# Inverse H transform of a spectral convolution on one core: one 128-column matmul per channel against two 64-column matmuls

## The chip, the cores and the metric

The kernel runs on one NeuronCore of a Trainium2 chip. The metric is device time in microseconds (us) of one execution, taken as the median of several. A profiled execution of the same program gives the trace from which all rows below come. The engines are called as the profile calls them: PE is TensorE's matmul side and PEld its weight loads, DVE is VectorE, ACT is ScalarE, POOL is GpSimd, SP is the engine that issues the large transfers.

## The reference

The input `x` has shape (4, 128, 128, 768) in float32: 4 images of 128 by 128 pixels with 768 channels. The channels form 8 blocks of 96. What is computed, cut to what matters:

```python
xf = jnp.fft.rfft2(x, axes=(1, 2), norm='ortho')          # over H and W
...                                                         # per block of 96 channels, complex:
o1r = relu(xr @ w1[0] - xi @ w1[1] + b1[0]); o1i = relu(xi @ w1[0] + xr @ w1[1] + b1[1])
o2r = o1r @ w2[0] - o1i @ w2[1] + b2[0];     o2i = o1i @ w2[0] + o1r @ w2[1] + b2[1]
o2r, o2i = softshrink(o2r, 0.01), softshrink(o2i, 0.01)
out = jnp.fft.irfft2(o2r + 1j * o2i, s=(H, W), axes=(1, 2), norm='ortho') + x
```

## The kernel before

The work is cut into 32 units, which this text calls images: one unit is one of the 4 input images with one block of 96 channels. All transforms are matmuls against cosine and sine tables held in `tab`. A loop of 16 steps runs over pairs of units; inside a step the two units (`p` = 0 and 1) are written out one after the other. Every engine has its own program, and semaphores alone tie them together.

For each unit PE goes through four stages in a fixed order that is written out by hand:

- **Forward lines** (`forward_lines`, lines 434 and 435): one matmul against row 0 of the image (line 418), and then for each of the 96 channels the transform along W. The stationary operand is a channel's 128 by 127 slice, held in one of five `ring` buffers. It is already issued as two matmuls: columns 0 to 63 of the slice give output partitions 0 to 63, columns 64 to 126 give partitions 64 to 126.
- **Mixing** (lines 468 to 561): the forward H transform (`fwd_big`, line 468, whose stationary operands have 128 columns, and `fwd_small`, line 480, which writes two halves of 64 partitions), the two complex products with ReLU between them, bias and softshrink on DVE. Near its end `keep_warm` (line 567) issues a few matmuls whose result nobody reads.
- **Inverse lines** (`inverse_lines`, line 447): for each of the 96 channels the inverse transform along H. The stationary operand is a channel's 128 by 128 slice in a `ring` buffer, the moving operand is the table `inv_h` of 128 columns. This stage is what the change touches.
- **Rows** (`rows`, lines 574 and 577): the inverse transform along W, 13 groups of two matmuls with up to 480 moving columns.

The 96 channels of a line stage are cut into 26 groups: 22 of 4 channels, then 3, 2, 2 and 1. One group fills one PSUM bank. For every group three things happen. ACT or DVE packs the channels from `ydg` into a `ring` buffer (ACT line 632, DVE line 767; the first five groups by ACT line 657 and, for the first 12 slots, DVE line 894). PE then multiplies and raises `line_done` on the group's last matmul. ACT or DVE moves the bank back into `ydg` (ACT line 638, DVE line 773). PE waits before group g for its pack, and from group 8 on for the move of group g - 8; a pack of group g waits for PE's group g - 5. After the last group `lines_moved` makes PE wait until all moves are done, since `rows` reads all of `ydg`. In the rows stage DVE (lines 839, 848 and 855) and POOL (line 926) add the results to the image, and SP stores them as they come and then loads the image after next into the same buffer.

In the program's rows each matmul of float32 stands once, while the trace shows it as two LDWEIGHTS and two MATMUL records. So 32 units of 96 channels make 6144 records of a kind.

Of the kernel before, what the change touches and what calls it, by code (L numbers as in the profile page):

```python
# [17 lines left out]
HALF = 64  # L18
# [16 lines left out]
RING = 5  # L35
# [6 lines left out]
def packer_h(g):  # L42
    return "act" if g < RING or g % 3 == 2 else "dve"
# [8 lines left out]
def upto(owner, g, who):  # L52
    return sum(owner(i) == who for i in range(g + 1))
# [124 lines left out]
def build(nc, x, mix, table, out):  # L178
    with ExitStack() as ctx:
        def sb(name, shape, dt=F32):  # L180
            return ctx.enter_context(nc.sbuf_tensor(name, shape, dt))
# [27 lines left out]
        ring = [sb(f"ring{j}", [128, CG, 128]) for j in range(RING)]  # L209
        ps = ctx.enter_context(nc.psum_tensor("ps", [128, 8, 512], F32))  # L210
# [53 lines left out]
        def mat(name):  # L264
            a, b = COLS[name]
            return tab[:, a:b]
# [17 lines left out]
        def line_bank(stage, g):  # L284

            return (g + ROW0_BANK + 1) % 8 if stage == 0 else g % 8
# [7 lines left out]
        def wait_moved(engine, q, stage, g):  # L294
            who = mover(stage, g)
            engine.wait_ge(line_sems[who], moved_count(q, stage, g, who))
# [70 lines left out]
        with nc.Block() as block:  # L367
# [46 lines left out]
            def _(pe):  # L414
# [23 lines left out]
                def inverse_lines(q):  # L438
                    for g in range(NG):
                        if g >= 8:  # L440
                            wait_moved(pe, q, 1, g - 8)
                        who = packer_h(g)
                        pe.wait_ge(pack_sems[who], PACKED_H[who] * q + upto(packer_h, g, who))
                        if g < RING:
                            pe.wait_ge(tail_packed, RING * q + g + 1)
                        for j in range(LINE_GROUPS[g][1]):
                            mm = pe.matmul(ps[:, line_bank(1, g), j * 128:(j + 1) * 128], ring[g % RING][:, j, :],  # L447
                                           mat("inv_h"), start=True, stop=True)
                        mm.then_inc(line_done, 1)

                def lines_moved(q, stage):
# [131 lines left out]
                with pe.Fori(0, STEPS) as t:  # L583
                    for p in range(PAIRS):
# [31 lines left out]
                        merge(q)  # L616
                        keep_warm(q, 3)
                        inverse_lines(q)
                        lines_moved(q, 1)
                        for g in range(NF):  # L620
# [327 lines left out]
```

## Time and profile before

| | |
|---|---|
| runs | 5172.28 us median of 3 (5172.27 to 5175.37) |
| profiled execution, its own time | 5172.48 us |
| its span from the first to the last instruction | 5170.2 us |
| PE busy | 5031.5 us, 97% of the span |
| PEld busy | 4143.5 us, 80% |
| DVE busy | 3993.2 us, 77% |
| ACT busy | 2508.0 us, 49% |
| POOL busy | 627.2 us, 12% |
| mean granted TensorE clock | 0.999 |

Busy time of PE is the union of matmul records. Records overlap (one begins before the one ahead of it has ended), so that a busy engine can still have its work done faster; what counts is the distance from one start to the next.

### The profile page before, as it was taken

What the parts mean: (1) busy time and instruction counts of PE and PEld (TensorE: products, weight loads), DVE (VectorE), ACT (ScalarE), POOL (GpSimd) and SP (SyncE); (2) the same over time, 40 slices, a digit from 0 to 9 for tenths busy, and PEclk for the clock granted to TensorE, in tenths of its full rate; (3) what the DMA queues carried; (4) which work ended last, traced back from release to release, by engine and by line L of the source; (5) the groups of instructions that cost most, each with busy time, mean ns of one, the idle gap of its engine ahead of it and who ended that gap; (6) DMA issues with size and microseconds to landing.
All of it is one profiled execution on the core that took longest, in us unless ns stands there. A gap on an engine that the chain in (4) does not pass through costs nothing.

```text
span 5170.2 us, 111909 instructions
## 1 busy us (share of the span) xinstructions
PE 5031.5 (97%) x43072; PEld 4143.5 (80%) x43072; DVE 3993.2 (77%) x5987; ACT 2508.0 (49%) x3649; POOL 627.2 (12%) x420
## 2 busy tenths in 40 slices
PE   7999999999999999999999999999999999999999
PEld 6887878888787887878878887888878778887887
DVE  6778777787777877778777787777787777877777
ACT  4554544545455454554445544445445455454543
POOL 0111011110111101111011110011110111101111
PEclk9999999999999999999999999999999999999999
DMA  3331233312333113332133321333312333123311
GB/s 107 99 99 36 73 100 99 104 44 61 100 99 104 50 54 99 99 104 61 44 100 99 104 74 43 87 99 104 89 41 74 99 104 99 44 61 99 103 50 50
DMA packets 1067748, 421.11 MB, mean 81 GB/s; under 512 B 1064864, under 2 KB 1064992, under 8 KB 1067168
## 3 DMA queue, kind: packets, MB, share of 16 engines
q1 hardware_dynamic: 1062432, 411.63, 30.1%
q8 instruction: 382, 6.26, 0.5%
q10 hardware_dynamic: 4736, 1.60, 0.1%
q14 instruction: 198, 1.62, 0.1%
HBM read 210.26 MB, written 201.33 MB: 80 GB/s over the span
## 4 chain that ended last, share of the span: by engine, by line
issue 88%; POOL 12%; POOLq 0%; DVE 0%
POOL x L926 12%; POOLq L925 0%; POOLq L929 0%; DVE x L855 0%; POOLq L926 0%; POOLq L938 0%
## 5 line engine op out<-in xcount | busy, mean ns | idle before, releaser
L926 POOL TENSOR_TENSOR x<-shrink_or_v,x 128x480 f32<-128x480 f32 (+1 forms) x416 | 627.0, 1507 | 4534.8 <-DVE shrink_or_v L848 4494.8
L543 PE MATMUL ps<-wts,hbig 128*128 128x192 f32 x4160 | 734.9, 327 | 4.3
L820 DVE TENSOR_TENSOR shrink_or_v<-ps,wts 128x768 f32<-128x768 f32 (+1 forms) x544 | 501.0, 921 | 281.5 <-PE ps L552 254.7
L773 DVE COPY ydg<-ps 128x512 f32<-128x512 f32 (+5 forms) x768 | 504.5, 657 | 250.8 <-PE ps L447 151.8
L447 PE MATMUL ps<-tab,ring 128*128 128x128 f32 x6144 | 694.6, 276 | 0.0
L447 PEld LDWEIGHTS ps<-tab,ring 128*128 128x128 f32 x6144 | 688.5, 192 | 5.4 <-DVE ring L894 5.4
L543 PEld LDWEIGHTS ps<-wts,hbig 128*128 128x128 f32 x4160 | 671.4, 190 | 16.5 <-ACT hbig L688 13.7
L434 PE MATMUL ps<-tab,ring 128*64 128x128 f32 x6144 | 681.6, 274 | 2.4 <-ACT ring L628 2.4
L435 PE MATMUL ps<-tab,ring 128*63 128x128 f32 x6144 | 681.6, 274 | 0.0
L434 PEld LDWEIGHTS ps<-tab,ring 128*64 128x64 f32 x6144 | 672.2, 137 | 7.3 <-ACT ring L628 4.2
L435 PEld LDWEIGHTS ps<-tab,ring 128*63 128x63 f32 x6144 | 672.1, 136 | 0.0
L638 ACT COPY ydg<-ps 127x512 f32<-127x512 f32 (+5 forms) x896 | 504.9, 573 | 344.2 <-PE ps L435 173.4
L665 ACT COPY zbig<-ps 128x512 f32<-128x512 f32 (+1 forms) x544 | 308.8, 568 | 613.6 <-PE ps L468 611.2
L468 PEld LDWEIGHTS ps<-tab,ydg 128*128 128x128 f32 x4032 | 506.1, 191 | 105.5 <-issue 84.3
L468 PE MATMUL ps<-tab,ydg 128*128 128x128 f32 x4032 | 567.4, 282 | 19.2 <-DVE ydg L773 17.7
L798 DVE TENSOR_TENSOR zlo<-zbig,zhi 128x1024 fp32r<-128x1024 f32 (+1 forms) x320 | 326.2, 1019 | 258.0 <-ACT zhi L672 258.0
L830 DVE TENSOR_TENSOR ydg<-shrink_or_v 128x768 f32<-128x768 f32 (+2 forms) x544 | 489.3, 899 | 17.8
L688 ACT ACTIVATE hbig<-ps,wts 128x1024 f32<-128x1024 f32 (+1 forms) x320 | 305.5, 955 | 310.0 <-PE ps L526 310.0
L628 ACT COPY ring<-x 128x508 f32<-128x508 f32 (+1 forms) x416 | 435.0, 1080 | 9.2 <-PE ps L435 9.2
L679 ACT CAST zsmall_hi<-ps 128x512 fp32r<-128x512 f32 (+1 forms) x320 | 163.1, 510 | 564.1 <-PE ps L480 564.1
L574 PE MATMUL ps<-ydg,tab 128*128 128x480 f32 (+1 forms) x832 | 396.0, 558 | 14.8 <-DVE ydg L773 14.8
L577 PE MATMUL ps<-ydg,tab 128*128 128x480 f32 x832 | 402.9, 566 | 0.0
(71 smaller groups left out, 7507.0 us busy)
## 6 DMA issues: line engine op xcount, KB each, us to landing
out<-x SPq DMA_DIRECT2D x352, 480.0 KB, 4.6
x<-in_x SPq DMA_DIRECT2D x192, 768.0 KB, 7.9
x<-in_x SPq DMA_DIRECT2D x32, 816.0 KB, 8.1
x<-in_x SPq DMA_DIRECT2D x32, 720.0 KB, 6.4
out<-x SPq DMA_DIRECT2D x32, 432.0 KB, 4.2
wts<-in_mix SPq DMA_DIRECT2D x16, 513.0 KB, 3.6
out<-x SPq DMA_DIRECT2D x32, 240.0 KB, 4.4
out<-x SPq DMA_DIRECT2D x32, 192.0 KB, 4.3
```

The lines of the kernel that those rows point to most:

```text
L434: pe.matmul(o[0:HALF], slot[:, 0:HALF], mat("fwd_w"), start=True, stop=True)
L435: mm = pe.matmul(o[HALF:127], slot[:, HALF:127], mat("fwd_w_odd"), start=True, stop=True)
L447: mm = pe.matmul(ps[:, line_bank(1, g), j * 128:(j + 1) * 128], ring[g % RING][:, j, :], mat("inv_h"), start=True, stop=True)
L468: mm = pe.matmul(ps[:, z_bank(u, h), k * H:(k + 1) * H], t[:, s:s + 2, :].rearrange("p k c -> p (k c)")[:, 0:BIG], mat("fwd_h"), start=Tru ...
L543: mm = pe.matmul(o, hbig[:, k * H:(k + 1) * H], mix_part("w2_big"), start=first, stop=False, skip_group_check=True)
L577: pe.matmul(ps[:, bank, 0:HG * CB], mat("inv_w_even"), ydg[:, HG * g:HG * g + HG, :].rearrange("p h c -> p (h c)"), start=True, stop=True) ...
L628: act.copy(*line_pack_moves(p, g)).then_inc(line_packed_act, 1)
L638: act.copy(*line_moves(stage, g)).then_inc(line_act, 1)
L773: dve.tensor_copy(*line_moves(stage, g)).then_inc(line_dve, 1)
L820: dve.tensor_tensor(parts(v), d, b2, ALU.add).then_inc(bias_done, 1)
L830: dve.tensor_tensor(dst, parts(v)[:, :, first:ne, :], parts(c)[:, :, first:ne, :], ALU.subtract).then_inc(shrunk, 1)
L926: pool.tensor_tensor(xs[p][:, a:b, :], ucopy[g % 4][:, 0:b - a, :], mirror(xs[p], a, b), ALU.add).then_inc(plus_ready, 1)
```

## The change

Each channel's matmul of the inverse H transform is issued as two: columns 0 to 63 of the channel's slice as the stationary operand, with output partitions 0 to 63 of the bank, and columns 64 to 127 with output partitions 64 to 127. Both read the same moving operand, the whole table `inv_h`. The semaphore is raised by the group's last matmul, as before. No other line changes; from the next line on, line numbers are one higher.

```diff
                         if g < RING:
                             pe.wait_ge(tail_packed, RING * q + g + 1)
                         for j in range(LINE_GROUPS[g][1]):
-                            mm = pe.matmul(ps[:, line_bank(1, g), j * 128:(j + 1) * 128], ring[g % RING][:, j, :],
-                                           mat("inv_h"), start=True, stop=True)
+                            for half in (slice(0, HALF), slice(HALF, 128)):
+                                mm = pe.matmul(ps[half, line_bank(1, g), j * 128:(j + 1) * 128],
+                                               ring[g % RING][:, j, half], mat("inv_h"), start=True, stop=True)
                         mm.then_inc(line_done, 1)
```

How the rows of PE's program stand at the place where the stage begins, behind the unread matmuls (`ps<-tab`), in the kernel before; "64x128" is output partitions by moving columns, and a count stands where rows repeat:

```order
L567 MATMUL ps<-tab 128x128 [waits zsmall_ready]
L567 MATMUL ps<-tab 128x128 x2
L443 ISA
L445 ISA [waits packed_act]
L447 MATMUL ps<-tab,ring 128x128 [waits tail_packed]
L447 MATMUL ps<-tab,ring 128x128 x3
```

The same place of PE's program after the change:

```order
L568 MATMUL ps<-tab 128x128 [waits zsmall_ready]
L568 MATMUL ps<-tab 128x128 x2
L443 ISA
L445 ISA [waits packed_act]
L448 MATMUL ps<-tab,ring 64x128 [waits tail_packed]
L448 MATMUL ps<-tab,ring 64x128 x7
```

The first group's 4 matmuls of 128 output partitions are 8 of 64 now, and the waits stand where they stood. At the end of the stage PE's program reads in the kernel before (the last group has one channel, and the row behind it begins the rows stage):

```order
L443 REGISTER_ALU [waits line_dve]
L447 MATMUL ps<-tab,ring0 128x128 [waits packed_dve]
L453 REGISTER_ALU
L453 REGISTER_ALU [waits line_act]
L574 MATMUL ps<-ydg,tab 128x384 [waits line_dve]
```

And after the change:

```order
L443 REGISTER_ALU [waits line_dve]
L448 MATMUL ps<-tab,ring0 64x128 [waits packed_dve]
L448 MATMUL ps<-tab,ring0 64x128
L454 REGISTER_ALU
L454 REGISTER_ALU [waits line_act]
L575 MATMUL ps<-ydg,tab 128x384 [waits line_dve]
```

Here too one matmul has become two between the same waits.

## Rows read from the trace of the kernel before

**Rows 1.** The page's parts 1 and 3: engines' busy time, and DMA queues.

```profile
PE 5031.5 (97%) x43072; PEld 4143.5 (80%) x43072; DVE 3993.2 (77%) x5987; ACT 2508.0 (49%) x3649; POOL 627.2 (12%) x420
...
q8 instruction: 382, 6.26, 0.5%
```

**Rows 2.** Groups by line, whole run: xcount | busy us, mean ns | idle before.

```profile
L447 PE MATMUL ps<-tab,ring 128*128 128x128 f32 x6144 | 694.6, 276 | 0.0
...
L434 PE MATMUL ps<-tab,ring 128*64 128x128 f32 x6144 | 681.6, 274 | 2.4 <-ACT ring L628 2.4
L435 PE MATMUL ps<-tab,ring 128*63 128x128 f32 x6144 | 681.6, 274 | 0.0
```

**Rows 3.** Timeline of PE, inverse lines of one unit: start us, us, what.

```profile
311.16 0.83 PE L567 MATMUL ps<-tab 128*128 128x128 f32 x6
311.96 21.70 PE L447 MATMUL ps<-tab,ring 128*128 128x128 f32 x192
334.13 0.59 PE L574 MATMUL ps<-ydg,tab 128*128 128x384 f32 x1 [0.46 <-DVE ydg L773]
```

**Rows 4.** Timeline of PE, the next unit's forward lines, begin and end.

```profile
355.55 0.32 PE L434 MATMUL ps<-tab,ring 128*64 128x128 f32 x1
355.56 0.32 PE L435 MATMUL ps<-tab,ring 128*63 128x128 f32 x1
355.71 0.27 PE L434 MATMUL ps<-tab,ring 128*64 128x128 f32 x1
...
376.46 0.27 PE L435 MATMUL ps<-tab,ring 128*63 128x128 f32 x1
377.29 0.37 PE L468 MATMUL ps<-tab,ydg 128*128 128x128 f32 x1 [0.56 <-DVE ydg L773]
```

**Rows 5.** Timeline of PE in mixing: 128 columns, then halves of 64, then 128.

```profile
378.84 0.50 PE L468 MATMUL ps<-tab,ydg 128*128 128x128 f32 x3
379.26 1.09 PE L480 MATMUL ps<-tab,ydg 128*64 128x128 f32 x16
380.29 0.49 PE L468 MATMUL ps<-tab,yedge 128*128 128x128 f32 x2
```

**Rows 6.** Timeline of DVE and ACT where the inverse lines begin.

```profile
311.71 0.66 DVE L894 COPY ring<-ydg 128x48 f32<-128x48 f32 x5 [0.15 <-ACT ydg L726]
...
314.79 1.10 ACT L632 COPY ring<-ydg 128x512 f32<-128x512 f32 x1
```

**Rows 7.** Timeline of DVE where the inverse lines end.

```profile
333.04 1.04 DVE L773 COPY ydg<-ps 128x256 f32<-128x256 f32 x2 [0.43 <-PE ps L447]
```

**Rows 8.** Windows, both line stages: PE, PEld, DVE, ACT, POOL busy, clock, DMA share, GB/s.

```profile
311.96:334.13 22.17, 21.71 (x193) 21.51 (x192) 16.69 (x31) 16.20 (x24) 0.00 (x0) 1.00 0.09 26
355.55:377.29 21.74, 21.18 (x386) 20.93 (x385) 17.17 (x31) 15.94 (x25) 2.96 (x2) 1.00 0.97 249
```

**Rows 9.** Waits, whole run: us in total, times, longest us.

```profile
ACT ydg L638 <- PE ps L447: 170.8, 256, 1.1
DVE ydg L773 <- PE ps L447: 151.8, 288, 1.7
...
PE ps L574 <- DVE ydg L773: 14.8, 32, 0.5
...
PE ps L418 <- DVE shrink_or_v L848: 1.6, 9, 0.2
```

**Rows 10.** Timeline of PE, starts of the stage in three other units (windows cut the counts).

```profile
152.17 1.05 PE L447 MATMUL ps<-tab,ring 128*128 128x128 f32 x7
...
472.46 0.71 PE L447 MATMUL ps<-tab,ring 128*128 128x128 f32 x4
...
632.27 0.94 PE L447 MATMUL ps<-tab,ring 128*128 128x128 f32 x6
```

## The prediction

> **What bounds the kernel now.** I read the page first: PE is busy 97% of the span, the next engine, DVE, 77% [rows 1]. PE being busy doesn't say that it couldn't go faster, so I went to the groups by line and then to the timeline of PE through one unit. The reader is to see there that the inverse lines are one unbroken run of 192 records over 21.70 us, and that over all 32 units PE was idle before them for 0.0 us [rows 2, 3]. The waits say the same from the other side: within this stage it is the movers that wait for PE, ACT 170.8 us and DVE 151.8 us in total, some 5 us per unit each [rows 9]. The windows agree: of the stage's 22.17 us DVE works 16.69 and ACT 16.20 [rows 8]. So the stage lasts as long as PE takes to issue its matmuls, plus a tail: the stage's last move ends, and only then PE begins the rows (0.46 us idle, waiting for DVE line 773) [rows 3, 7]. What PE saves in the stage is time saved, as long as nobody else becomes late by it.
>
> **What the change costs and gives.** It takes 6144 matmul records of 128 stationary columns away and puts 12288 of 64 columns in their place; each still streams 128 moving columns. No DMA, no work of DVE, ACT, POOL or SP is added or moved.
>
> The kernel before holds nearly the same code: the forward lines do 96 channels as pairs of 64 and 63 stationary columns out of the same ring, against a table of 128 columns. There the two halves start 0.01 us apart and run beside each other, so a pair costs about one slot of time and not two [rows 4]. The run goes from 355.55 to the end of its last record, 376.46 + 0.27 = 376.73: 21.18 us, for the same 96 channels that take 21.70 us as whole matmuls [rows 3, 4]. Difference 0.52 us per unit.
>
> I want to know where this comes from, since a difference between two stages could be due to something else in them. Forward: the second pair starts at 355.71, 0.16 after the first, and the last of the 192 pairs about at 376.45, so the other 190 steps take 20.74 us: 0.1092 each [rows 4]. Inverse: the last record starts some 0.275 before the end (mean duration 276 ns [rows 2]), at 21.43 into the run. Its first step is not seen alone in that row, but line 468 in mixing has the same shape, and there two records of a run that starts unprepared last 0.49 us together, so that the second starts 0.49 - 0.275 = 0.21 after the first [rows 5]. That leaves 21.22 us for 190 steps: 0.1117 each. So the pair saves 2.5 ns in each of 190 steps, 0.47 us, and 0.05 us in the first step.
>
> Could the tables matter? The forward pairs use two different tables and the inverse pairs one table twice. Line 480 in mixing has that form: 16 records, 8 pairs against one table, in 1.09 us [rows 5]. With 0.16 for the first step, 6 steps of 0.109 and a last record of 0.28 it comes to 1.09. The pair's step is the same. The one column that the forward's second half lacks (63 against 64) is also complete there, and costs nothing that shows.
>
> **The entry.** PE now goes from whole matmuls (the unread ones) to halves, and back at the end; before, it did neither here. Mixing shows what such a turn costs: the last of line 468's records starts at 378.84 + 0.50 - 0.275 = 379.06, the first half-width one at 379.26, that is 0.20 later where a step of 0.11 would be usual [rows 5]. At the entry of the inverse lines the last unread matmul starts at 311.16 + 0.83 - 0.275 = 311.71 and the first inverse one at 311.96, already 0.25 later [rows 3]. What holds it is DVE's first tail pack: five of them take 0.66 us from 311.71 on, so that the first is done near 311.91 [rows 6]. The turn's 0.20 us lies under that wait; it would be exposed by some 0.2 us only if the two came one after the other. I take nothing for the entry; bounds 0 and 0.09 us (0.20 less the usual 0.11).
>
> The Trainium skill says of the same thing, in "TensorEngine Tiling (Array Packing)", section "Key Properties", that changing the tiling mode drains the engine, which speaks against a change that adds two such turns per unit. The trace agrees that such a turn costs time (0.20 us against 0.11 [rows 5]). If both were paid in full on top of the waits, the sum would shrink to the case "both turns exposed" below.
>
> **The exit.** From halves to whole: the last line 480 record starts at 379.26 + 1.09 - 0.27 = 380.08, the first whole one at 380.29, 0.21 later [rows 5]. At the end of the inverse lines PE stands idle for 0.46 us anyway until DVE has moved the last bank [rows 3], so the turn is hidden. The last half starts 0.01 us behind its partner, and the last move can begin only then: a loss of 0.01 us. The forward stage has a longer tail, 377.29 - 376.73 = 0.56 us [rows 4], of which 0.1 us more than the inverse stage's. It is followed by other waits in the program (row 0's transfer, the edges), so I count it against nothing, but as the pessimistic bound of the tail I take it whole: 0.10 us.
>
> **Who becomes late.** The closest of the packs is ACT's first, for group 5: it ends at 314.79 + 1.10 = 315.89 [rows 6]. PE needs it after 40 records: today at 311.96 + 0.21 + 39 x 0.1117 = 316.53 for the matmul and about 0.11 earlier for its weights, 316.42. After the change at 311.96 + 0.05 + 39 x 0.109 = 316.27 for the weights. 0.38 us are left of 0.53. From then on a stage shorter by 0.5 us has to fit DVE's 16.69 and ACT's 16.20 us into 21.65, while the forward stage already fits 17.17 and 15.94 into 21.74 with 2.4 us of PE idle in the whole run [rows 2, 8]. The wait behind the stage moves with it: rows begin when the last bank is moved, and DVE's chain of the rows stage, for which PE's line 418 waits (1.6 us in all [rows 9]), begins with the first row matmul. Stores and loads are released by the same chain and shift as a whole. Nothing in the loop is tied to a time of its own, so the saving of a unit is a saving of the run.
>
> **The sum.** 21.70 - 21.18 = 0.52, less 0.01 at the exit: 0.51 us per unit, x 32 = 16.3 us. From the profiled execution's own 5172.48 us (span 5170.2) this gives 5156.2, and from the median of 5172.28, which lies 0.2 below it, **5156.0 us**, a change of 0.32%. A measurement of this kernel can tell about 0.2%, 10.3 us, from no change. Bounds of the parts: entry 0 to 0.09, exit 0.01 to 0.10, together at worst 0.18 us of loss more, which is 5.8 us.
>
> **The rivals.**
> 1. Both turns exposed. The 0.20 us of a turn add themselves to the waits instead of lying under them. Gain 0.51 - 0.18 = 0.33 us per unit, 10.6 us: 5161.7. For it speaks that the first inverse record waits for a semaphore that its weight load carries; against it that in mixing the turn takes place with no wait at all, so it needs no semaphore to begin [rows 5]. Chance 0.07.
> 2. The pair runs at the whole matmul's step, 0.1117, because each half streams the same 128 columns and the step is set by something that a pair doesn't shorten. Only the first step's 0.05 us less the 0.01 of the exit stays, 1.3 us: 5171. Two stretches of the trace in this form run at 0.109 [rows 4, 5], which speaks against it. Chance 0.05.
>
> The same page's section "Theoretical Speedup" gives a gain only where a dimension is 64 or less, and a whole 128 by 128 slice cut in two has none; by that the time would be rival 2's. The trace disagrees, if only by 2.5 ns per step.
>
> 3. ACT or DVE become late in the stage: pack 5 has 0.38 us left. If another unit's early packs came later than in the one read, PE would wait part of its saving away. The idle time of 0.0 us over 32 units [rows 2] says that no unit comes near. Gain halved, 8 us: 5164. Chance 0.03.
> 4. Slower: PE runs out of instructions. Instructions are themselves brought in while the kernel runs (6.26 MB on one queue [rows 1]), and the inverse lines follow mixing, which is dense already, while the forward lines, with the same density as the new stage, follow the sparse rows stage and may live on what was fetched during it. A place where the supply breaks off is the turn of the loop: a unit takes 311.96 - 152.17 = 159.79 us, one with the turn in it 472.46 - 311.96 = 160.50, the next 632.27 - 472.46 = 159.81 [rows 3, 10], so a turn costs 0.7 us. One such stall per inverse stage would give 0.7 - 0.51 = 0.2 us of loss per unit, 6 us: 5178, and two 5201. It decides from 0.51 us per unit on. Against it: the forward stage keeps the density for 21 us while DMA is 97% busy, whereas in the inverse stage it is 9% [rows 8]. Chance 0.03.
>
> **How the numbers follow.** The forecast has 0.82, rivals 0.07, 0.05, 0.03 and 0.03. The range of 5153 to 5162 holds the forecast, with 3 us below it for parts that the reading in hundredths of a us hides (0.1 us per unit), and rival 1 above: 0.89 of the cases, of which I believe 0.8 after errors of my own reading. Faster by over 0.2% are the forecast and, at the very bound, half of rival 1: 0.85. Within 0.2%: the other half, rival 2 and rival 3, 0.12. Slower: 0.03.
>
> **What would show it.** The line's matmul group should be 12288 records, still with no idle time ahead of it, of about 273 ns; a run of them in one unit about 21.2 us long, with starts of pairs 0.109 apart; its first start 0.25 after the last unread matmul's start, as now; and the rows' wait for DVE at 0.46 to 0.48 us. All other stages keep their lengths: a unit takes 159.3 and 160.0 us in turn. The prediction is wrong if the pair's step is not that of the forward lines, if the entry grows, or if idle time appears in front of a later stage by as much as this one lost.

## The result, and the profile after

| | before | after |
|---|---|---|
| median | 5172.85 us (5171.31 to 5175.37, 8 runs) | 5156.97 us (5156.48 to 5158.11, 8 runs) |
| profiled execution | 5172.48 us, span 5170.2 | 5156.87 us, span 5154.6 |

The ratio is 0.9969, with a 95% interval of 0.9958 to 0.998: 15.9 us less. The forecast was 5156.0 with a range of 5153 to 5162.

The groups by line of after, whole run, answer to [rows 2]; the columns are the same.

```profile
L434 PE MATMUL ps<-tab,ring 128*64 128x128 f32 x6144 | 681.8, 273 | 2.8 <-ACT ring L629 2.8
L435 PE MATMUL ps<-tab,ring 128*63 128x128 f32 x6144 | 681.8, 273 | 0.0
L448 PE MATMUL ps<-tab,ring 128*64 128x128 f32 x12288 | 677.8, 273 | 0.0
L448 PEld LDWEIGHTS ps<-tab,ring 128*64 128x64 f32 x12288 | 670.1, 137 | 5.4 <-DVE ring L895 5.4
```

Line 448 is the old line 447. It has twice the records and 16.8 us less busy time (694.6 before), and still no idle time ahead of it. Its busy time per unit is now the forward lines' 21.18 us.

The timeline of PE in the same unit as [rows 3]:

```profile
310.81 0.83 PE L568 MATMUL ps<-tab 128*128 128x128 f32 x6
311.62 21.18 PE L448 MATMUL ps<-tab,ring 128*64 128x128 f32 x384
333.27 0.91 PE L575 MATMUL ps<-ydg,tab 128*128 128x384 f32 x2 [0.47 <-DVE ydg L774]
```

The reader is to see three distances. From the last unread matmul's start (310.81 + 0.83 - 0.275 = 311.37) to the first half it is 0.25 us, as before. The run is 21.18 us long and not 21.70. The idle time in front of the rows is 0.47 us and not 0.46.

The starts of the stage in the two units behind it answer to [rows 10] (windows cut the counts):

```profile
471.53 0.66 PE L448 MATMUL ps<-tab,ring 128*64 128x128 f32 x8
...
630.82 0.88 PE L448 MATMUL ps<-tab,ring 128*64 128x128 f32 x12
```

From one stage to the next it is 471.53 - 311.62 = 159.91 us with the loop's turn in it and 159.29 without; before it was 160.50 and 159.81.

The waits of after, where they answer to [rows 9], with two that are small:

```profile
ACT ydg L639 <- PE ps L448: 156.3, 256, 1.0
...
DVE ydg L774 <- PE ps L448: 141.0, 288, 1.6
...
PE ps L418 <- DVE shrink_or_v L849: 2.6, 12, 0.3
```

The movers wait for PE 25.3 us less than before (170.8 + 151.8 against 156.3 + 141.0), and still wait for it: PE bounds the stage as it did.

### The profile page after: what moved, and what is told of

Same layout as the page of the kernel before. It is cut to its first block, busy times and chain, and to the rows that moved or that the text cites. A ratio compares the mean times of both kernels' runs of the same rounds, so it can differ in the third digit from the quotient of the medians.

```text
span 5154.6 us, 124197 instructions
## 1 busy us (share of the span) xinstructions
PE 5015.0 (97%) x49216; PEld 4124.6 (80%) x49216; DVE 3992.1 (77%) x5987; ACT 2507.4 (49%) x3649; POOL 627.3 (12%) x420
## 4 chain that ended last, share of the span: by engine, by line
issue 88%; POOL 12%; POOLq 0%; DVE 0%
POOL x L927 12%; POOLq L926 0%; POOLq L930 0%; DVE x L856 0%; POOLq L927 0%; POOLq L939 0%
## 5 line engine op out<-in xcount | busy, mean ns | idle before, releaser
L774 DVE COPY ydg<-ps 128x512 f32<-128x512 f32 (+5 forms) x768 | 504.4, 657 | 240.0 <-PE ps L448 141.0
L434 PE MATMUL ps<-tab,ring 128*64 128x128 f32 x6144 | 681.8, 273 | 2.8 <-ACT ring L629 2.8
L434 PEld LDWEIGHTS ps<-tab,ring 128*64 128x64 f32 x6144 | 671.5, 137 | 8.5 <-ACT ring L629 4.8
L448 PE MATMUL ps<-tab,ring 128*64 128x128 f32 x12288 | 677.8, 273 | 0.0
L448 PEld LDWEIGHTS ps<-tab,ring 128*64 128x64 f32 x12288 | 670.1, 137 | 5.4 <-DVE ring L895 5.4
```

The costliest lines, as they stand in the source:

```text
L434: pe.matmul(o[0:HALF], slot[:, 0:HALF], mat("fwd_w"), start=True, stop=True)
L448: mm = pe.matmul(ps[half, line_bank(1, g), j * 128:(j + 1) * 128], ring[g % RING][:, j, half], mat("inv_h"), start=True, stop=True)
L774: dve.tensor_copy(*line_moves(stage, g)).then_inc(line_dve, 1)
```

## The experiments

Two questions were open behind a forecast that came true. Why is a pair of halves 2.5 ns faster than a whole matmul (theory A: a whole's step is set by loading 128 stationary columns; theory B: a fixed cost in each pass)? And does the turn from whole to half matmuls cost something that DVE's wait only hides? Each run was timed beside the kernel before on its own chip; that kernel's median was 5174.6 us beside e1 to e4, 5173.3 beside e5 to e8 and 5173.4 beside e9 to e12. e1, e2, e5, e6 and e7 stand on one execution each, the others on five or more.

**e1: one half alone.** The kernel of after, where the upper half of each channel's slots is not computed in this stage:

```diff
-                            for half in (slice(0, HALF), slice(HALF, 128)):
+                            for half in (slice(0, HALF),):
```

> The kernel of after with only the first half (columns 0 to 63) of each channel issued in the inverse lines; the second half's output is left out. Theory A (a whole record's step of 0.1117 us is set by loading its 128 stationary columns, a half's step of 0.109 by streaming its 128 moving columns, so that a second half beside the first costs nothing): one half alone still steps at 0.109, the stage is 21.17 us and the kernel at 5157 us, within 1 us. Theory B (there is a fixed cost of 2.5 ns in each of the two passes of a record, and a pair hides one of them by overlap): a half alone has nothing beside it and steps at 0.1117, the stage is 21.65 us, the kernel near 5172 us. Theory C (the two halves take turns and share the step): the stage falls clearly below 21 us, until DVE with 16.7 us of work in it bounds it.

5157.38 us. The timeline of PE in e1:

```profile
311.55 21.18 PE L448 MATMUL ps<-tab,ring 128*64 128x128 f32 x192
```

Half the records take the same 21.18 us. The second half of after costs nothing, and the step of a lone half is already the short one. This is A's number; B wanted 21.65 and C less than 21.

**e2: whole matmuls, 96 moving columns.** The kernel of before; 32 of the 128 columns of each channel's result are left out:

```diff
-                            mm = pe.matmul(ps[:, line_bank(1, g), j * 128:(j + 1) * 128], ring[g % RING][:, j, :],
-                                           mat("inv_h"), start=True, stop=True)
+                            mm = pe.matmul(ps[:, line_bank(1, g), j * 128:j * 128 + 96], ring[g % RING][:, j, :],
+                                           mat("inv_h")[:, 0:96], start=True, stop=True)
```

> The kernel of before (whole matmuls) with 96 of the 128 moving columns in the inverse lines; the other 32 columns of each channel's result are left out. Theory A (the load of 128 stationary columns sets the step): the step stays at 0.1117 us and the stage at 21.7 us, the kernel at 5172 us. Theory B (streaming plus 2.5 ns in each of two passes): the step is 0.080 + 0.005 = 0.085 us, a group of 4 channels takes 0.68 us, and the stage goes down until DVE and ACT bound it, to 17 to 18 us; the kernel gets 120 to 150 us faster.

5173.22 us. The timeline of PE in e2:

```profile
312.24 21.68 PE L447 MATMUL ps<-tab,ring 128*128 128x96 f32 x192
```

A quarter of the streaming is gone and the stage is 0.02 us shorter. Streaming does not set the step of a whole matmul of 128 columns.

**e5: halves, 96 moving columns.** The same cut in the kernel of after:

```diff
-                                mm = pe.matmul(ps[half, line_bank(1, g), j * 128:(j + 1) * 128],
-                                               ring[g % RING][:, j, half], mat("inv_h"), start=True, stop=True)
+                                mm = pe.matmul(ps[half, line_bank(1, g), j * 128:j * 128 + 96],
+                                               ring[g % RING][:, j, half], mat("inv_h")[:, 0:96], start=True, stop=True)
```

> The kernel of after (halves) with 96 of the 128 moving columns in the inverse lines; the other 32 columns of each channel's result are left out. Theory A (a whole's step is set by its load of 128 columns, a half's by streaming): the step falls to 0.080 + 0.0025 = 0.0825 us, where the whole matmuls stayed at 0.112 with the same 96 columns. PE would need 15.9 us for the stage, DVE and ACT have more than 16 in it, so the stage ends at 17 to 18 us and the kernel near 5157 - 32 x 3.7 = 5040 us. Rival (the halves' step is set by their own load or by the issue of four records): the step stays at 0.109 and the kernel at 5157.

5015.51 us. The timeline of PE in e5, in a unit that begins some 4 us earlier:

```profile
307.09 3.52 PE L448 MATMUL ps<-tab,ring 128*64 128x96 f32 x80
311.04 12.76 PE L448 MATMUL ps<-tab,ring 128*64 128x96 f32 x304 [0.43 <-ACT ring L633]
324.32 0.91 PE L575 MATMUL ps<-ydg,tab 128*128 128x384 f32 x2 [0.52 <-DVE ydg L774]
```

The second run of 304 records, 152 pairs, takes 12.76 us; less the last record of 0.25 and a first step of some 0.13, that leaves 12.38 us for 150 steps, 0.0825 us, the number expected. The same cut that gave whole matmuls nothing gives halves a quarter. The stage is 17.23 us; PE runs into a wait of 0.43 us for ACT's pack 5. The expected 5040 was too careful: DVE and ACT held PE up there once, and not for the rest of the stage. The pack is the one that the prediction named as the closest.

Taken together, e1, e2 and e5 leave only theory A of the three: the step of a whole matmul is the load of its 128 columns, 0.112 us, and that of a half is its streaming, 0.109 us with 128 moving columns and 0.0825 with 96. The experiments vary the streaming and not the load alone, but the rows of the weight loads show the load. In the kernel before, and in e7 (quarters, below):

```profile
L447 PEld LDWEIGHTS ps<-tab,ring 128*128 128x128 f32 x6144 | 688.5, 192 | 5.4 <-DVE ring L894 5.4
```

```profile
L448 PEld LDWEIGHTS ps<-tab,ring 128*32 128x32 f32 x24576 | 673.1, 110 | 36.0 <-issue 28.4
```

The mean record is 110 ns for 32 columns, 137 for 64 (the result's rows above) and 192 for 128: 27 ns more for 32 columns, 55 for 64. That is 0.85 ns a column and, as an estimate from these rows, 0.11 us for 128, the step of a whole matmul.

**e3 and e4: 6 unread matmuls instead of 3**, in the kernel of before and of after:

```diff
-                        keep_warm(q, 3)
+                        keep_warm(q, 6)
```

> The kernel of before with 6 unread matmuls ahead of the inverse lines instead of 3, so that DVE's tail pack is done before PE is through with them. Both theories: the first inverse record follows the last unread one by one step, 0.11 us, and its own step is 0.11 instead of 0.21: 6 records of 0.1117 are added (0.67 us), 0.14 of waiting and 0.10 of the first step are saved: 0.43 us per unit, 13.8 us, 5186 to 5187.

> The kernel of after with 6 unread matmuls instead of 3. Theory (the turn from whole to half matmuls costs 0.20 us from start to start and lies under DVE's wait in the kernel of after): the turn is exposed now. First half 0.20 after the last unread start, so 0.67 - 0.05 = 0.62 us more per unit, 19.8 us, 5176.8; the gain over the whole matmuls with 6 unread ones falls from 16 to about 9.5 us. Rival (a turn costs nothing, and what mixing shows at line 480 is something else): the first half follows after 0.11, 0.53 us more per unit, 5173.9, gain 12.4 us. Second rival (the turn is already paid on top of the wait in the kernel of after): gain stays near 16 us or grows.

e3 5187.48 us (ratio 1.0025, 1.0015 to 1.0035), e4 5177.69 us (1.0006, 0.9996 to 1.0016). The timeline of PE in e3:

```profile
311.86 1.50 PE L567 MATMUL ps<-tab 128*128 128x128 f32 x12
313.20 3.07 PE L447 MATMUL ps<-tab,ring 128*128 128x128 f32 x26
```

And in e4:

```profile
312.11 1.50 PE L568 MATMUL ps<-tab 128*128 128x128 f32 x12
313.54 0.66 PE L448 MATMUL ps<-tab,ring 128*64 128x128 f32 x8
```

With DVE's wait out of the way the first whole record starts 313.20 - (311.86 + 1.50 - 0.275) = 0.11 us after the last unread one, the first half 313.54 - (312.11 + 1.50 - 0.275) = 0.20 us. So the turn is real, it costs 0.09 us, and in the kernel of after it lies wholly under the wait. Exposed, it cuts the gain from 15.9 to 9.8 us, where 9.5 was expected. That is not the turn alone: in e3 the first step of the whole matmuls has become short as well.

**e6: halves apart.** Within a group the lower halves of all its channels, and then the upper ones:

```diff
-                        for j in range(LINE_GROUPS[g][1]):
-                            for half in (slice(0, HALF), slice(HALF, 128)):
+                        for half in (slice(0, HALF), slice(HALF, 128)):
+                            for j in range(LINE_GROUPS[g][1]):
```

> The kernel of after with the halves in another order: within a group first the lower halves of all channels, then the upper ones. Theory (two halves run beside each other only when neighbours in the program use different columns of the array): each half takes a step of its own, but for the neighbours at the borders of runs. 384 records less some 51 borders, at 0.109, is 36.4 us, without the borders 41.9: the stage grows by 15 to 21 us, the kernel to 5640 to 5820. Rival (PE finds the partner in its queue by itself): 5157.

5248.49 us, a miss by over 390 us. The timeline of PE in e6: the stage's beginning in two windows that end at 314.774 and 314.79, and the whole run:

```profile
314.28 0.76 PE L448 MATMUL ps<-tab,ring 128*64 128x128 f32 x5
...
314.28 0.82 PE L448 MATMUL ps<-tab,ring 128*64 128x128 f32 x6
...
314.28 24.05 PE L448 MATMUL ps<-tab,ring 128*64 128x128 f32 x384
```

The group has 8 records of lower halves before the first of an upper half. Five have started by 314.774, and a sixth starts before 314.79, although a record of the same columns would follow 0.109 later, near 314.88. So, by this spacing, the first upper half begins beside the fifth lower one, ahead of three records that stand before it in the program. If all halves took their own steps, the stage would last 384 x 0.109 = 41.9 us; it lasts 24.05, 2.87 more than with neighbours paired, which is about one step of 0.11 for each of the 25 borders between groups. PE finds the partner by itself, at some steps' distance, and the order of halves matters far less than expected.

**e7: quarters.**

```diff
-                            for half in (slice(0, HALF), slice(HALF, 128)):
+                            for half in (slice(0, 32), slice(32, 64), slice(64, 96), slice(96, 128)):
```

> The kernel of after with four matmuls of 32 stationary columns per channel. Theory A: streaming 128 columns still sets the step, and the four quarters run beside each other, as they start 0.01 us apart: step 0.109, 5157 within 2 us, or up to 1 us per stage more for the later start of the last quarter. Rival (PE can't issue eight records in 0.109 us, or instructions don't come in fast enough with 24576 more of them): the step grows; at 0.02 us per record it would be 0.16, 10 us per unit, 5470.

5192.04 us, between the two. What the weight loads and the matmuls of line 448 wait for without a releaser, over the whole run of e7 (us in total, times, longest us):

```profile
PEld ps L448 <- issue: 28.4, 70, 0.9
PE ps L448 <- issue: 11.1, 39, 0.6
```

And one unit's timeline; its window begins behind the stage's first 8 records:

```profile
152.76 12.61 PE L448 MATMUL ps<-tab,ring 128*32 128x128 f32 x448
165.52 7.25 PE L448 MATMUL ps<-tab,ring 128*32 128x128 f32 x248 [0.16 <-issue]
172.93 1.96 PE L448 MATMUL ps<-tab,ring 128*32 128x128 f32 x64 [0.15 <-issue]
```

While it runs, it runs as theory A says: 448 records are 112 steps, and (12.61 - 0.27) / 111 = 0.111 us, with one short delay in it. But here PE stops, waiting for nothing that the profile shows: its weight loads 70 times for 28.4 us in all, its matmuls, which come out of the same stops later, 39 times for 11.1 us. The stage takes 22.26 us on average instead of 21.18, 34 us more in 32 units, which is nearly all of what e7 loses. No run of halves has such stops. They stand at fixed places: here behind record 8 + 448 = 456 of the stage and behind 456 + 248 = 704. In a unit of the loop's other half:

```profile
954.67 17.22 PE L448 MATMUL ps<-tab,ring 128*32 128x128 f32 x618
972.19 3.69 PE L448 MATMUL ps<-tab,ring 128*32 128x128 f32 x124 [0.30 <-issue]
976.06 1.07 PE L448 MATMUL ps<-tab,ring 128*32 128x128 f32 x26 [0.18 <-issue]
```

In all units of the first kind the stops are behind records 456, 580 or 704, in all of the other behind 370, 494, 618 or 742: multiples of 124 apart. The queue that brings instructions ([rows 1]) moves 526 packets in e7 and 430 in the kernel of after, 96 more for 12288 more MATMUL records, which is one packet for 128 of them. Within the stage its packets start 3.8 us apart in e7's trace (median over all units), while 124 records at full pace take 31 steps of 0.109, 3.4 us; in the kernel of after they start 7.0 us apart. All this fits the rival of the prediction that PE runs out of instructions; that it is what PE waits for is inferred, since the profile names no releaser.

**e8: turns merged.** With a turn priced at 0.09 us plus its first step, this run moves turns instead of adding them. Halves stand now also next to halves that were there: the forward H transform of iteration 0, the first part of iteration 1, all second parts, and the second product in the loop.

```diff
-                        mm = pe.matmul(ps[:, z_bank(u, h), k * H:(k + 1) * H],
-                                       t[:, s:s + 2, :].rearrange("p k c -> p (k c)")[:, 0:BIG], mat("fwd_h"),
-                                       start=True, stop=True)
+                        for part in ((slice(0, HALF), slice(HALF, BIG)) if u == 0 or h == 1 or (u, h) == (1, 0)
+                                     else (slice(0, BIG),)):
+                            mm = pe.matmul(ps[part, z_bank(u, h), k * H:(k + 1) * H],
+                                           t[:, s:s + 2, :].rearrange("p k c -> p (k c)")[:, part], mat("fwd_h"),
+                                           start=True, stop=True)
...
-                                mix2_whole(q, it - 2)
+                                mix2_whole(q, it - 2, (slice(0, HALF), slice(HALF, H)))
```

> The kernel of after, with halves also for the forward H transform's first iteration, for the first part of the second one and for every second part, and for the product behind them (the one of 192 moving columns) inside the loop, so that a turn from whole to half matmuls moves forward instead of being added, and one per unit falls away. Theory (turn 0.09 us and 0.05 us of first step, and 2.5 ns for each whole record of 128 moving columns replaced, none for those of 192, whose streaming of 0.160 us is longer than the load): 0.14 + about 90 records x 0.0025 = 0.36 us per unit, 11.7 us: 5145 to 5146. Rival (halves next to row-tiled or accumulating matmuls cost more than seen): at or above 5157.

5182.95 us (ratio 1.0018, 1.0009 to 1.0027), 37 us worse than expected. Two windows of e8 around the same wait in mixing, in two units; the columns are those of [rows 8], and the first number behind POOL is the granted clock:

```profile
223.00:227.00 4.00, 3.34 (x9) 2.28 (x9) 0.61 (x2) 0.00 (x0) 0.00 (x0) 0.69 1.08 295
383.00:387.00 4.00, 2.13 (x11) 1.61 (x9) 1.83 (x2) 0.99 (x3) 0.00 (x0) 1.00 1.17 325
```

And its timeline of PE in the first of them:

```profile
223.66 0.50 PE L497 MATMUL ps<-zhi,w1lo 128*128 128x512 f32 x1 [1.87 <-DVE zsmall_lo L805]
224.00 0.39 PE L498 MATMUL ps<-zhi,w1hi 128*128 128x512 f32 x1
...
225.68 0.63 PE L510 MATMUL ps<-zsmall_hi,w1lo 128*128 128x512 f32 x1
226.11 0.63 PE L511 MATMUL ps<-zsmall_hi,w1hi 128*128 128x512 f32 x1
```

PE sat idle for 1.87 us, and 0.85 us after it had begun again its matmuls took 0.43 us from start to start instead of 0.23: the clock stood at the 1.2 GHz level, which the window shows as 0.69 on average. It happened behind this wait in 19 of 32 units, which took 1.5 us longer; in the others it stayed at 2.4 GHz, though the wait is 1.87 us in all 32. In the kernel of after the same wait is 1.50 us and the clock never falls there. The edit had made PE arrive earlier at a result that DVE delivers when it does, and so made the wait longer.

**e9: e8 with 6 unread matmuls in that wait.**

```diff
+                            if it == 1:
+                                for i in range(6):
+                                    pe.matmul(ps[:, SMALL_BANK, 0:H], mat("inv_h"), mat("fwd_h"), start=True, stop=True)
                             if it >= 1:
                                 mix1_whole(q, it - 1)
```

> The kernel of run e8 (turns merged) with 6 more unread matmuls (12 records of 128 columns, 1.3 us) in PE's wait of 1.87 us for the first remainder of DVE, line 805 there. In e8 19 of 32 units had the clock at 1.2 GHz for 3.4 us right behind that wait and took 1.5 us longer; the others took 0.21 us less than in the kernel of after. Theory (the longer idle time let the clock fall, and nothing else is wrong with e8): granted clock back at 0.999 and all units 0.21 us shorter than after's, 5149 to 5151. Rival (the fall has another cause, as the halves themselves): the clock falls again and the time stays near 5180.

5156.66 us (ratio 0.9967, 0.9955 to 0.9979), the clock back at 0.999, 26.3 us less than e8. The 26 us were the fall of the clock. But of the 6.7 us that were expected beyond the gain of after, next to nothing came. The waits of e9 say where it stopped:

```profile
DVE x L764 <- issue: 29.4, 27, 2.4
...
PE ps L471 <- DVE zsmall_lo L808: 5.9, 13, 1.0
```

And the timeline of DVE in e9:

```profile
391.15 1.06 DVE L764 TENSOR_TENSOR x<-x 128x864 f32<-128x864 f32 x1 [2.44 <-issue]
```

Line 764 is the first fold of the next image. The expectation of e12 takes this idle time for a wait for that image's first rows, but in the trace these had landed at 373.93, 17 us earlier. What stands there is the turn of DVE's own loop (line 921), between these two instructions:

```profile
L921 DVEq COMPARE_BRANCH  x1: 63/63/63, 387.5 to 387.5; - x1
L921 DVEq FUSED_REGOPS  x1: 62/62/62, 391.0 to 391.0; - x1
```

The first is the branch at the loop's end, the second the first instruction of the loop's body, 3.6 us later. e9's trace has 14 such turns of 2.8 to 3.6 us, and DVE's idle time in them is 25.4 us, most of the 29.4 above. The turn comes in every second unit. Behind it DVE has three folds to do, and the remainder for PE's line 471, which follows them, is late.

**e10: only the late merges**, iterations 2 to 6:

```diff
-                        for part in ((slice(0, HALF), slice(HALF, BIG)) if u == 0 or h == 1 or (u, h) == (1, 0)
+                        for part in ((slice(0, HALF), slice(HALF, BIG)) if h == 1 and u >= 2
```

> The kernel of e8 without its edits to the first two iterations: halves only in the second parts of iterations 2 to 6 of the forward H transform, and in the second product inside the loop. PE's wait for the first remainder is as in after, 1.5 us, so the clock stays at 0.999. Theory: 5 parts of 8 whole records become 8 steps of halves, 0.0025 us less each, 0.1 us per unit, 3 us: 5153 to 5155. Rival (the second product's halves, beside accumulating into the same bank, cost more): at or above 5157.

5158.07 us (ratio 0.997, 0.9958 to 0.9981), span of the profile 5154.6, the same as after's. The clock stayed up, as expected, but the 3 us didn't come; the interval is too wide to show 3 us, the trace is not. Units without DVE's loop turn are 0.1 us shorter, as expected (159.20 us from one stage to the next against 159.29), so the second product's halves cost nothing there. The other units lose it:

```profile
PE ps L471 <- DVE zsmall_lo L805: 8.8, 11, 1.3
```

In after's trace this wait is 0.4 us. DVE's first fold waits 34.5 us in all in e10's trace, where it is 25.9 in after's: the loop's turn took 3.4 us on average, and 2.8 in after. Why it took longer is not shown.

**e11: more turns.** The kernel of after, with halves in the first parts of iterations 2 to 9, which stand between row-tiled and whole matmuls:

```diff
-                        mm = pe.matmul(ps[:, z_bank(u, h), k * H:(k + 1) * H],
...
+                        for part in ((slice(0, HALF), slice(HALF, BIG)) if h == 0 and u >= 2 else (slice(0, BIG),)):
```

> The kernel of after with halves also in the first part of iterations 2 to 9 of the forward H transform, which stands between row-tiled and whole matmuls. There each block gives 8 x 0.0025 us and adds a turn from halves to whole: 0.09 us of start and 0.10 of first step, less the 0.05 that a first step of halves is shorter. Theory (an uncovered turn costs that): 8 blocks x 0.12 = 1.0 us per unit, 31 us: 5185 to 5190. Rival (turns are free where no wait stands, only halves' steps count): 8 x 0.02 us less per unit, 5152.

5188.17 us (ratio 1.0028, 1.0017 to 1.0038), 31 us above after, as expected. The timeline of PE in e11:

```profile
413.00 1.09 PE L470 MATMUL ps<-tab,ydg 128*64 128x128 f32 x16
414.03 0.50 PE L496 MATMUL ps<-zhi,w1lo 128*128 128x512 f32 x1
414.36 0.39 PE L497 MATMUL ps<-zhi,w1hi 128*128 128x512 f32 x1
```

And the same place in the timeline of after:

```profile
410.17 1.16 PE L469 MATMUL ps<-tab,ydg 128*128 128x128 f32 x8
411.09 0.47 PE L495 MATMUL ps<-zhi,w1lo 128*128 128x512 f32 x1
411.40 0.39 PE L496 MATMUL ps<-zhi,w1hi 128*128 128x512 f32 x1
```

From block to block it is 1.03 us with halves and 0.92 with whole matmuls, though the halves' own run is shorter (1.09 against 1.16), and 0.02 more come in the next step: some 0.12 us for each of 8 blocks.

**e12: e9 with DVE's folds one iteration later.**

```diff
-FOLD_IN = {1: (0, 1, 2), 2: (3,), 3: (4,), 4: (5,), 5: (6,)}
+FOLD_IN = {1: (), 2: (0, 1), 3: (2,), 4: (3,), 5: (4,), 6: (5,), 7: (6,)}
```

> The kernel of run e9 (turns merged, 6 more unread matmuls) with DVE's folds of the next image later: none in mixing iteration 1, the first two in iteration 2, one in each from 3 to 7. In e9 the odd units of the profile took the expected 94.70 us for mixing, the others, for which the image is loaded right behind the loop's turn, 95.14 in the middle and up to 95.77: DVE idles up to 2.4 us at its first fold (line 764 there, waiting for the image's first rows), is late with the remainder that PE's line 471 waits for, and PE idles up to 1.0 us. Theory (the load of the next image eats what the shorter mixing gives): with the first fold 10 us later the wait is gone, all units take 94.70 us, 16 x 0.43 = 7 us less than e9: 5149 to 5151. Rival (the even units lose by something else, or DVE is too full behind iteration 2 to take the folds): within 2 us of e9's 5157, or above, with PE waiting for DVE in later iterations.

5154.34 us (ratio 0.9963, 0.995 to 0.9977). This is 2.3 us less than e9, where 7 were expected. Both waits of e9's rows above are gone from e12's trace. It was the folds behind the turn that made the remainder late; the load was not the cause. DVE's turn is still there (3.1 us on average), but what follows it now waits for ACT anyway. Mixing takes 94.87 us in nearly every unit, where e9 had 94.70 in its good units and 95.14 in the middle of the others. The 0.17 us arise at one place, where PE's weight load for line 471 waits in 31 units:

```profile
PEld ps L471 <- DVE zsmall_lo L808: 12.1, 31, 0.4
```

In iteration 2 DVE has two folds ahead of that remainder now. In one unit e12's remainder ends at 569.49 and the weight load starts at 569.54, while in e9 it had ended 1.6 us before the load. The fix has moved part of the loss. The interval takes in after's ratio of 0.9969, so that e12 is the lowest time of the kernels that compute the whole result, but not shown to be faster than the kernel of after.

## Why the prediction was right

- *The pair's step.* Forecast 0.1092 us from the forward lines and line 480; the stage's run is 21.18 us as read there, to the hundredth. The step was right, and that the inverse stage would have it too.
- *Its reason.* The prediction read 2.5 ns per step and gave no cause. e1, e2 and e5 give it: a whole matmul is held by its weight load, a half by its streaming. Rival 2 rested on the opposite, that both are set by streaming 128 columns. The speed-up rule of the Trainium skill's "TensorEngine Tiling (Array Packing)", section "Theoretical Speedup", counts only how full the array is, and misses this gain.
- *The entry*, taken at nothing because DVE's first tail pack covers the turn: right (0.25 us before and after), and e3 and e4 show the other half of the claim, that there is something to cover: 0.09 us. Rival 1 fails on the same rows.
- *The exit*, 0.01 us: right (0.47 against 0.46).
- *Who becomes late.* Nobody in the stage, as forecast; e5 shows that pack 5 is the first to be, once each step takes 0.027 us less.
- *The sum.* Per unit the stage gives 22.17 - 21.65 = 0.52 us by the timeline's hundredths, and 0.51 were forecast, 16.3 us in 32 units. The profiled spans differ by 15.6 and the medians by 15.9. Over 32 units 0.52 us are 16.6, so 1.0 us of the spans is missing. Outside the stage PE waits 1.0 us more at line 418 (2.6 against 1.6) and 0.4 at line 434 (2.8 against 2.4), and 0.6 less for DVE at line 469: 0.8 us more, most of it. That all else would shift as a whole was nearly right, not quite.
- *The slower rival*, that instructions run out: not at halves. e7 shows stops that look like it at twice their density.
- *"Nothing in the loop is tied to a time of its own."* This was too strong, though it did no harm. The prediction priced the loop's turn on PE alone (0.7 us). DVE has one too, 2.8 us from branch to next instruction on average in after's trace, in the middle of mixing. Time saved in the inverse lines gets past it. Of the time saved in mixing, e9 and e10 lose theirs behind it, in every second unit.

## What to carry to other kernels

A matmul that has full use of the array can still be bound by the load of its stationary operand: compare the distance between starts with what the same shape takes with fewer moving columns, and if it doesn't fall, split the stationary operand in column halves. Price each turn between whole and half matmuls (here 0.09 us and a longer first step) and put it where PE waits anyway; uncovered, eight of them cost twice what this change gave. Before making PE faster in front of a wait, ask what fills the wait then: 0.37 us more of idle time cost 26 us here. And when an engine idles without a releaser, look for its loop's branch before blaming a transfer.

## What the runs showed of the hardware that I had not expected

- A second column half costs nothing at all: 192 and 384 records take the same 21.18 us (e1).
- PE starts a half beside an earlier one over three records that stand between them in the program (e6). The Trainium skill says in "TensorE: Matmul & The Clock Gate", section "The mechanism", that matmuls start strictly in the order of the program; for halves in different columns this trace disagrees.
- The clock fell to the 1.2 GHz level behind an idle time of 1.87 us in 19 of 32 units, and behind none of 1.50 us (e8 and the kernel of after).
- With quarters the stage grew by 34 us in 32 units through stops without a releaser in the profile, at places 124 records apart (e7).
- The turn of DVE's loop takes 2.8 us or more from the branch to the next instruction (2.8 us on average in the kernel of after, 3.4 in e10), and it is idle time without a releaser.
